# Spreading the B and C rows of the selective scans by TensorE instead of DMA, and moving the first block's injections

## The chip, the cores and the metric

The kernel runs on one core of a Trainium2 chip. Its engines are TensorE (PE), VectorE (DVE), ScalarE (ACT), GpSimd (POOL) and SyncE (SP, which only issues DMAs here). They run their own instruction streams and wait for each other by semaphores. The metric is the device time of one execution in microseconds, as a median over runs.

## The reference, cut to what matters

Two layers over 2048 tokens of width 128. The change touches the second layer's bidirectional Mamba block (inner width 256, 16 states, two directions "f" and "b"), which is computed side by side with that layer's attention and its mixture of eight experts.

```python
u, z = split(x @ Win.T); u = silu(causal_conv4(u)); dtr, B, C = split(u @ Wx.T)
dt = softplus(dtr @ Wdt.T + bdt)
# for each token t, channel d (256) and state n (16), in each direction:
h[d, n] = exp(dt[t, d] * A[d, n]) * h[d, n] + (dt[t, d] * u[t, d]) * B[t, n]
y[t, d] = sum_n h[d, n] * C[t, n]  +  u[t, d] * D[d]
out     = (y * silu(z)) @ Wout.T
```

B and C are 16 rows each per token, the same for all 256 channels.

## The kernel before

Three stages run one after the other: layer 0, the front stage (attention of the second layer, and the inputs of the Mamba block, which go to DRAM as dt, dt*u, u, z and the rows B, C), and the tail (the scans, the experts and the sums of all).

**The scans.** Tokens are cut into chunks of 512 (`CH`); two directions give 8 chunks n (`NN`). A scan tile is 128 partitions = 4 states x 32 channels, by 512 tokens. Input i = (n, b) is a chunk and a half b of the channels. Each i has 4 rounds (q = 0 to 3, a group of four states) of 4 tiles (j = 0 to 3, 32 channels). Tile k has r = k // 4 as its round. Per tile: ACT writes the decay exp(dt*A) into one of four PSUM banks (`spread_decay`); POOL makes the injection (dt*u)*B, two tiles at a time, into a ring of four (`inject`); DVE scans (L1709); the result is multiplied by C (`weigh`, on DVE, or on POOL for the tiles that `on_pool` names); ACT copies the last column of each tile for the next chunk (`keep`); PE adds the four states (`sums`, L1829), with a lag: the weighing of round r waits for the sums of round r - 2. The last chunk of each direction has nothing to keep. Round 0 to 3 (input 0) run at the end of the front stage as the "early" block; rounds r = 4 to 63 are the tail.

**B and C.** The row set m = 4n + q has four rows of B and four of C. Each must be on 32 partitions, to match the tile. `Inputs.load_bc` does that with 8 broadcast DMAs of 64 KB (L419) into one of five slots (`NBC`) of `bs` and `cs`. The row sets 0 to 4 are loaded in the front stage, the others in the tail, in rounds with r % 8 >= 4, for the chunk that follows. All are issued by SP, in program order with the loads of dt (L405), of dt*u (L405 too), of u and z (L411), of the experts' weights (L1359 to L1363) and the stores of their results (L1367). The inputs dt and dt*u of i + 1 are issued at the first round of i, once their buffer (two are used in turn) is free; SP stands behind each wait.

**Beside the scans.** PE and ACT share three PSUM banks (`ring`) for everything else: transposes and matmuls of the experts (T, H, Y), the projection of a chunk (O), and at the start of the tail the normed rows (N), the router's logits (L) and counts (C). A use takes the bank of the third use before it, once that was emptied. The order of the uses is one list over the rounds (`uses_beside`); ACT or DVE empties two to three rounds later, at fixed tiles.

**The start of the tail.** DVE adds the attention's output and takes its statistics, ACT standardizes 16 token tiles (`standardize`, L1479), PE turns them, ACT applies gain and bias (`normed`), PE makes logits, DVE chooses experts (`choose`) and places tokens (`place`), and POOL scatters rows by indirect DMA, one per two scan tiles (rounds 12 to 19). In these rounds and in 56 to 63 POOL weighs no tiles.

**The early block.** In the attention, unit u (0 to 255; 16 units make a step s) is: scores on PE, two exponentials on ACT (L853), weights times values on PE. DVE finds the maxima of a later step's scores beside it (L881). At the end of a step's maxima POOL splits them into three parts (`split_max`, L710 to L716), PE turns them, DVE copies them (`place_rows`, L895) and SP stores them into the queries (L597); the step's first scores wait for that. The maxima end at u = 234; from U0 = 235 the early block is scanned: POOL injects (L727), DVE scans (L941) and weighs (L949), POOL keeps (L733), PE sums (L1116). Its injections share two buffers, so that each waits for scans.

## Time and profile before

| | us |
|---|---|
| median of 3 runs | 1341.69 (1341.12 to 1343.34) |
| the profiled execution | 1339.88 |
| its span, first to last instruction | 1338.2 |
| DVE busy | 1205.2 (90%) |
| PE busy | 976.8 (73%) |
| ACT busy | 867.7 (65%) |
| POOL busy | 499.4 (37%) |
| tail stage | 883 to 1338 |

Busy shares are means over stages with different limits. A stage is read by stretches, and a stall by what ended it. Times of events are microseconds from the start of the span.

### The profile page before, as it was taken

The page shows a single profiled execution, that of the slowest core. Times are in us where ns is not written, and L with a number is a line of the kernel's source. Part 1 is how long each engine was busy: PE and PEld are TensorE (multiplying, and loading weights), DVE is VectorE, ACT ScalarE, POOL GpSimd, SP SyncE. Part 2 cuts the span into 40 slices and gives each one's busy share as a digit, 9 for nine tenths or more (in the row PEclk, how much of TensorE's full clock was granted, in tenths as well). Part 3 has the DMA queues.
Part 4 walks back from the last instruction along what each step waited for, and adds up shares of the span by engine and source line. Part 5 has one row for each costly group of instructions (what it writes and reads, how often), then busy time and mean ns, then how long its engine had stood idle before and what let it go on. Part 6 is the DMA issues. An engine that isn't in the chain of part 4 may idle for free. (4 is left out here: it accounts for less than half of the span.)

```text
span 1338.2 us, 18056 instructions
## 1 busy us (share of the span) xinstructions
PE 976.8 (73%) x5909; PEld 319.3 (24%) x5909; DVE 1205.2 (90%) x1759; ACT 867.7 (65%) x1298; POOL 499.4 (37%) x353
## 2 busy tenths in 40 slices
PE   2789996888888888888888888855433676767443
PEld 1443321111111111111111111122101344434111
DVE  7882667999999999999999999958999998989997
ACT  6445557777777777787877887757344655656531
POOL 5030113300000000000000012747698998988994
PEclk9889996999999999999999999885656867777565
DMA  3034333200000033000001100036467888797731
GB/s 100 0 129 151 132 126 128 73 1 1 1 29 18 12 64 64 29 24 16 7 17 33 33 17 1 2 88 162 85 151 152 192 215 199 181 210 183 190 81 34
DMA packets 88863, 111.47 MB, mean 83 GB/s; under 512 B 15603, under 2 KB 46122, under 8 KB 88770
## 3 DMA queue, kind: packets, MB, share of 16 engines
q1 hardware_dynamic: 87746, 108.22, 31.2%
q0 software_dynamic: 1024, 2.10, 0.6%
q8 instruction: 47, 0.77, 0.2%
q14 instruction: 46, 0.38, 0.1%
HBM read 84.43 MB, written 25.56 MB: 82 GB/s over the span
## 5 line engine op out<-in xcount | busy, mean ns | idle before, releaser
L881 DVE TENSOR_REDUCE at_mpart<-psum 128x1 f32<-128x512 f32 x1024 | 637.8, 684 | 44.1 <-PE psum L1058 40.9
L853 ACT ACTIVATE at_probs<-psum 128x1024 f32<-128x1024 f32 x512 | 495.3, 1021 | 146.4 <-PE psum L1088 145.6
L1453 POOL TENSOR_TENSOR t_inject<-shared 128x1024 f32<-128x1024 f32 x120 | 281.0, 2353 | 56.4 <-DVE psum L1709 23.5
L1101 PE MATMUL psum<-at_probs,at_vg 128*32 128x512 f32 x2048 | 276.5, 612 | 0.9 <-ACT at_probs L853 0.9
L1058 PE MATMUL psum<-at_ks,at_qs 56*128 56x512 bf16 x1024 | 203.1, 393 | 100.3 <-DVE at_mpart L881 99.6
L710 POOL CAST at_m<-at_mneg 128x16 bf16<-128x16 f32 x16 | 4.0, 251 | 574.5 <-DVE at_mneg L886 567.6
L1515 ACT ACTIVATE psum<-shared,aneg 128x512 f32<-128x512 f32 x240 | 164.5, 691 | 70.2 <-DVE t_hc L1641 56.5
L1829 PE MATMUL psum<-t_hc,stack 128*32 128x512 f32 x480 | 98.6, 906 | 137.7 <-DVE t_hc L1641 102.7
L1709 DVE TENSOR_TENSOR_SCAN psum<-psum,last,t_inject 128x512 f32<-128x512 f32 x149 | 184.0, 1273 | 1.1 <-ACT psum L1515 1.1
L1088 PE MATMUL psum<-at_qs,at_ks 59*128 59x512 bf16 x1024 | 157.9, 382 | 9.4 <-ACT at_probs L853 5.2
L1058 PEld LDWEIGHTS psum<-at_ks,at_qs 56*128 56x128 bf16 x1024 | 49.3, 93 | 424.5 <-DVE at_mpart L881 409.9
L1641 DVE TENSOR_TENSOR t_hc<-psum,shared 128x512 f32<-128x512 f32 (+1 forms) x121 | 112.9, 933 | 0.0
L1527 ACT ACTIVATE last<-psum 128x1 f32<-128x1 f32 x128 | 21.1, 165 | 137.4 <-DVE t_hc L1641 134.7
L1439 POOL TENSOR_TENSOR t_hc<-t_hp,shared 128x512 f32<-128x512 f32 x59 | 74.5, 1272 | 4.0 <-DVE t_hp L1709 3.9
L1088 PEld LDWEIGHTS psum<-at_qs,at_ks 59*128 59x128 bf16 x1024 | 50.3, 96 | 60.3 <-ACT at_probs L853 27.9
L1709 DVE TENSOR_TENSOR_SCAN t_hp<-psum,last,t_inject 128x512 f32<-128x512 f32 x43 | 54.6, 1270 | 9.2 <-ACT psum L1515 7.8
L1030 PE MATMUL psum<-mp_xm,mp_taps 128*128 128x512 f32 x128 | 62.7, 641 | 0.0
L696 POOL TENSOR_TENSOR shared<-shared 128x1024 f32<-128x1024 f32 x8 | 22.3, 2802 | 98.6 <-DVE shared L933 98.6
L1829 PEld LDWEIGHTS psum<-t_hc,stack 128*32 128x32 f32 x480 | 13.3, 134 | 190.2 <-issue 145.4
L1101 PEld LDWEIGHTS psum<-at_probs,at_vg 128*32 128x32 f32 x2048 | 40.5, 108 | 63.2 <-issue 60.1
L1783 PE MATMUL psum<-t_xT,t_w 128*128 128x128 f32 x184 | 36.4, 361 | 22.7 <-ACT t_xT L1486 21.2
L1824 PE MATMUL psum<-shared,diag 128*32 128x512 f32 x120 | 25.5, 937 | 21.1 <-DVE t_gated L1652 21.1
(248 smaller groups left out, 987.0 us busy)
## 6 DMA issues: line engine op xcount, KB each, us to landing
shared<-mp_dt_d SPq DMA_DIRECT2D x64, 256.0 KB, 5.9
shared<-mp_dtu_d SPq DMA_DIRECT2D x64, 256.0 KB, 9.3
shared<-mp_bc_d SPq DMA_DIRECT2D x256, 64.0 KB, 2.1
t_w<-in_w SPq DMA_DIRECT2D x46, 256.0 KB
mp_u_d<-shared SPq DMA_DIRECT2D x8, 512.0 KB, 4.8
mp_z_d<-shared SPq DMA_DIRECT2D x8, 512.0 KB, 4.6
mp_dt_d<-shared SPq DMA_DIRECT2D x8, 512.0 KB, 2.8
mp_dtu_d<-shared SPq DMA_DIRECT2D x8, 512.0 KB, 2.7
```

The lines of the kernel that those rows point to most:

```text
L853: act.activation(probs[:, u_ % 2, p, :], s_pair[p], ACT.Exp, scale=float(HD) ** -0.5).then_inc(probs_ready, 1)
L881: dve.reduce_max(mpart[:, s % 2, 2 * jp + b, i, kc:kc + 1], ring[x % 3], AX.X).then_inc(ring_free, 1)
L1030: mm = pe.matmul(out, S.taps[:, d, i, P * b:P * (b + 1)], xm[:, n % 2, i:i + CH], start=(i == 0), stop=(i == KC - 1))
L1058: pe.matmul(ring[z_ % 3], qs[half(b, DQ), buf, of_pair(jp, c * CH + i * P, P)], ks[half(b, DQ), buf, of_pair(jp, kc * CH, CH)], start=True ...
L1088: mm = pe.matmul(s_banks[p][b], ks[half(b, DM), g % 2, of_pair(p, kt * P, P)], qs[half(b, DM), g % 2, of_pair(p, c * CH, CH)], start=True, ...
L1101: mm = pe.matmul(o_bank[VW * j:VW * (j + 1), :], vg[:, g % 2, kt, j, :], probs[:, u_ % 2, j // 2, CH * (j % 2):CH * (j % 2 + 1)], start=(k ...
L1439: pool.tensor_tensor(hc[:, r % 2, j, :], hp[:, by_pool[k] % NHP, :], cs[:, (NQ * (i // NB) + q) % NBC, :], ALU.mult).then_inc(pool_weighed, 1)
L1453: pool.tensor_tensor(inject[:, k % NI:k % NI + 2, :], dus[:, i % 2, j:j + 2, :], bs[:, m % NBC, :].unsqueeze(1).to_broadcast([P, 2, CH]), ...
L1515: act.activation(decay[k % ND], dts[:, i % 2, j, :], ACT.Exp, scale=S.aneg[:, n // NCH, m:m + 1])\
L1641: dve.tensor_tensor(hc[:, r % 2, j:j + n, :], decays[:, j:j + n, :], cs[:, m % NBC, :].unsqueeze(1).to_broadcast([P, n, CH]), ALU.mult).th ...
L1709: dve.tensor_tensor_scan(h, decay[k % ND], inject[:, k % NI, :], last[:, k % PC:k % PC + 1] if n % NCH else 0.0, ALU.mult, ALU.add).then_i ...
L1829: mm = pe.matmul(y_bank[GC * j:GC * (j + 1), :], S.stack[:, :], hc[:, r % 2, j, :], start=False, stop=(q == NQ - 1), tile_position=(0, GC ...
```

## The change

In the front stage the early injections get eight buffers of their own (parts of buffers that are no longer used), and POOL makes them ahead, after the maxima of steps 12, 13 and 14. DVE's early scans and weighings are placed anew, and so are PE's early sums.

In the tail one DMA per chunk loads the 32 rows of B and C onto 32 partitions (`bc_rows`). PE multiplies them with a 0/1 matrix (`sel`, built once by POOL) into a bank of the ring, for B and for C of each row set (key S), and ACT copies the bank into the slot of `bs` or `cs` two rounds later. SP's broadcasts and their waits go; ACT waits instead for the slot to be free, and POOL and DVE wait for ACT's copy. In rounds 4 to 11 POOL also weighs tile 3 of the rounds where it did not. Several steps at the start of the tail come one tile later, and the scatters two tiles.

```diff
         first = Inputs(S)
+        early_in = [vg_all[:, 0:2 * CH], vg_all[:, 2 * CH:4 * CH]]
+        early_in += [t.rearrange("p k f -> p (k f)") for t in (S.taps[:, 0, :, :], S.taps[:, 1, :, :])]
+        early_in += [t.rearrange("p n f -> p (n f)")[:, 0:2 * CH] for t in (S.w_in[:, :, :], xm[:, :, :])]
+        early_in = [t.rearrange("p (j t) -> p j t", t=CH) for t in early_in]
+        early_in += [first.dts[:, 0, 0:2, :], first.dts[:, 0, 2:4, :]]
...
-        early_in = vg_all[:, 0:NJ * CH].rearrange("p (j t) -> p j t", t=CH)
...
         LAST_CONST = 2 + 2 * NB + SP4 + 1
+        EARLY_PAIRS = (0, 1), (2, 3, 4), (5, 6, 7)
...
                     pool.wait_ge(first_in[6 + q], 16 * 2 * SP4)
-                if p >= 2:
-                    pool.wait_ge(e_scanned, 2 * p - 2)
-                pool.tensor_tensor(early_in[:, j:j + 2, :], first.dus[:, 0, j:j + 2, :],
+                if p == 2:
+                    pool.wait_ge(prep_free, len(STEPS))
+                if p == 6:
+                    pool.wait_ge(e_decay, NE0)
+                pool.tensor_tensor(early_in[p], first.dus[:, 0, j:j + 2, :],
...
             for s in range(1, NSTEP):
-                if s == NSTEP - 1:
-                    for p in range(2):
+                if s >= NSTEP - 3:
+                    for p in EARLY_PAIRS[s - NSTEP + 3]:
...
                 early_keep(p)
-                if p + 2 < NE0 // 2:
-                    early_inject(p + 2)
...
                     dve.wait_ge(e_injected, k + 1)
-                    dve.tensor_tensor_scan(tile, tile, early_in[:, k % NJ, :], 0.0, ALU.mult, ALU.add).then_inc(e_scanned, 1)
+                    dve.tensor_tensor_scan(tile, tile, early_in[p][:, k % 2, :], 0.0, ALU.mult, ALU.add).then_inc(e_scanned, 1)
...
                     maxima(n)
-                if U0 <= u_ <= U0 + NE0 and (u_ - U0) % 2 == 0:
-                    p = (u_ - U0) // 2
-                    if p < NE0 // 2:
-                        early_scan(p)
-                    if p:
-                        early_weigh(p - 1)
+                if u_ == U0:
+                    early_scan(0)
+                    early_scan(1)
+                if u_ == U0 + 3:
+                    early_weigh(0)
+                if U0 + 3 <= u_ < U0 + 3 + NE0 - 4 and (u_ - U0 - 3) % 2 == 0:
+                    early_scan((u_ - U0 - 3) // 2 + 2)
+                    early_weigh((u_ - U0 - 3) // 2 + 1)
+                if u_ == U0 + 3 + NE0 - 4:
+                    early_weigh(NE0 // 2 - 1)
...
                     maxima(n)
-                if U0 + 7 <= u_ < U0 + 7 + 4 * NQ and (u_ - U0 - 7) % 4 == 0:
-                    early_sums((u_ - U0 - 7) // 4)
+                if u_ - U0 in (7, 11, 14, 17):
+                    early_sums((7, 11, 14, 17).index(u_ - U0))
...
             r, j = divmod(k, NJ)
-            return not SCATTER <= r < SCATTER + MOVE and not GATHER <= r < GATHER + MOVE and (j == 0 or j == 3 and r % 3 == 1)
+            return not SCATTER <= r < SCATTER + MOVE and not GATHER <= r < GATHER + MOVE and (j == 0 or j == 3 and (r % 3 == 1 or r < SCATTER))
...
 
+        def spread_at(r):
+
+            m = r // 8 * NQ + r % 8
+            return m if r % 8 >= 4 and NBC <= m < NN * NQ else None
+
         def uses_beside(r):
             keys = []
+            if (m := spread_at(r)) is not None:
+                keys += [("S", m, 0), ("S", m, 1)]
...
         hn2 = sb("hn2", [P, NCH, CH])
+        bc_rows, sel = sb("bc_rows", [BC, 2, CH]), sb("sel", [BC, 2 * NQ, P])
...
         dt_in, du_in, uz_in = ([sem(f"{n}_in{p}") for p in range(2)] for n in ("dt", "du", "uz"))
-        bc_in = [sem(f"bc_in{p}") for p in range(NBC)]
+        bc_in, sel_ready = [sem(f"bc_in{p}") for p in range(2)], sem("sel_r")
...
         def _(sp):
-            def load_bc(m):
-                n0, q0 = divmod(m - NBC, NQ)
-                done = PC * n0 + PB + NJ * (q0 + 1)
-                sp.wait_ge(injected, done - K0)
-                sp.wait_ge(pool_weighed, by_pool[done])
-                sp.wait_ge(dve_weighed, by_dve[done // NJ])
-                feed.load_bc(S, sp, m, bc_in[m % NBC])
+            def load_bc(n):
+                d, c = divmod(n, NCH)
+                if n >= 3:
+                    sp.wait_ge(side_full, USE["S", NQ * (n - 2) + NQ - 1, 1] + 1)
+                sp.dma_start(bc_rows[:, n % 2, :], S.bc_d[d][:, cols(c)]).then_inc(bc_in[n % 2], 16)
...
 
+            load_bc(1)
             for r in range(R0, NR):
                 i, rest = divmod(r, NQ)
+                if r % 8 == 0 and r // 8 + 1 < NN:
+                    load_bc(r // 8 + 1)
                 if rest == 0 and 2 <= i + 1 < NN * NB:
                     load_steps(i + 1)
-                if NBC <= r // 8 * NQ + NQ + r % 8 - 4 < NN * NQ and r % 8 >= 4:
-                    load_bc(r // 8 * NQ + r % 8)
...
             def numbering():
+                pool.tensor_copy(sel[:, :, :].rearrange("r x (s g) -> r (x s) g", g=GC),
+                                 S.ident[0:BC, 0:BC].unsqueeze(2).to_broadcast([BC, BC, GC])).then_inc(sel_ready, 1)
...
                 if j == 0 and m >= NBC:
-                    pool.wait_ge(bc_in[m % NBC], 16 * 2 * SP4 * (m // NBC))
+                    pool.wait_ge(emptied["act"], EMPTIED[USE["S", m, 1]][1])
...
                 if k % 2:
-                    if SCATTER <= r < SCATTER + MOVE:
-                        scatter((k - SCATTER * NJ) // 2)
+                    if 2 <= k - SCATTER * NJ < 2 + 2 * NT:
+                        scatter((k - SCATTER * NJ - 2) // 2)
...
                         .then_inc(xn_ready, 1)
+
+            def spread_states(m, o):
+                full("S", m, o)
+                if o == 0:
+                    n0, q0 = divmod(m - NBC, NQ)
+                    done = PC * n0 + PB + NJ * (q0 + 1)
+                    act.wait_ge(injected, done - K0)
+                    act.wait_ge(pool_weighed, by_pool[done])
+                    act.wait_ge(dve_weighed, by_dve[done // NJ])
+                act.activation((bs, cs)[o][:, m % NBC, :], bank("S", m, o), ACT.Copy).then_inc(emptied["act"], 1)
...
                         turned(s)
+                if m < 2:
+                    if (x_ := spread_at(r - 2)) is not None:
+                        spread_states(x_, m)
...
-                if k in (K0 + 17, K0 + 20):
+                if k in (K0 + 17, K0 + 21):
                     normed(0 if k == K0 + 17 else 2)
                     normed(1 if k == K0 + 17 else 3)
-                if K0 + 11 <= k < K0 + 11 + NCH:
-                    standardize(k - K0 - 11)
+                if K0 + 12 <= k < K0 + 12 + NCH:
+                    standardize(k - K0 - 12)
...
                 if m >= NBC:
-                    dve.wait_ge(bc_in[m % NBC], 16 * 2 * SP4 * (m // NBC))
+                    dve.wait_ge(emptied["act"], EMPTIED[USE["S", m, 1]][1])
...
                     variances()
-                if k == K0 + 8:
+                if k == K0 + 9:
...
-                if k in (K0 + 20, K0 + 23):
-                    logits(0 if k == K0 + 20 else 2)
-                    logits(1 if k == K0 + 20 else 3)
-                if k == K0 + 24:
+                if k in (K0 + 21, K0 + 24):
+                    logits(0 if k == K0 + 21 else 2)
+                    logits(1 if k == K0 + 21 else 3)
+                if k == K0 + 25:
                     choose()
-                if K0 + 28 <= k < K0 + 31:
-                    place[k - K0 - 28]()
+                if K0 + 29 <= k < K0 + 32:
+                    place[k - K0 - 29]()
...
                 return ring[x % R]
+
+            def spread_states(m):
+                n, q = divmod(m, NQ)
+                for o in range(2):
+                    out = take("S", m, o)
+                    if o == 0:
+                        pe.wait_ge(bc_in[n % 2], 16 * ((n + 1) // 2 if n % 2 else n // 2))
+                        pe.wait_ge(sel_ready, 1)
+                    pe.matmul(out, sel[:, NQ * o + q, :], bc_rows[:, n % 2, :], start=True, stop=True).then_inc(side_full, 1)
...
                 sums(r)
+                if (m := spread_at(r)) is not None:
+                    spread_states(m)
```

## Rows read from the trace of the kernel before

**Rows 1.** The page: busy us, share of the span and instructions of each engine.
```profile
PE 976.8 (73%) x5909; PEld 319.3 (24%) x5909; DVE 1205.2 (90%) x1759; ACT 867.7 (65%) x1298; POOL 499.4 (37%) x353
```
**Rows 2.** Tail by stretches: length; PE, PEld, DVE, ACT, POOL busy; clock; DMA share; GB/s.
```profile
883.00:960.60 77.60, 36.99 (x190) 21.04 (x190) 66.91 (x112) 39.22 (x90) 56.57 (x38) 0.60 0.58 131
960.60:1018.73 58.13, 22.15 (x91) 4.39 (x92) 58.13 (x61) 26.66 (x64) 52.84 (x32) 0.53 0.56 132
1018.73:1266.13 247.40, 158.79 (x874) 88.06 (x872) 232.71 (x220) 144.00 (x394) 225.11 (x120) 0.74 0.83 196
```
**Rows 3.** The same view: rounds 27, 35, 43, 51 and, undisturbed, round 30.
```profile
1065.36:1073.48 8.12, 6.68 (x47) 4.75 (x46) 6.53 (x7) 5.15 (x12) 5.89 (x4) 0.97 0.97 241
1118.53:1129.01 10.48, 9.67 (x53) 6.73 (x53) 5.79 (x6) 6.33 (x18) 6.48 (x5) 0.74 0.96 228
1174.54:1184.56 10.02, 8.36 (x51) 6.18 (x51) 6.51 (x8) 7.20 (x21) 5.20 (x4) 0.80 0.94 219
1230.61:1239.79 9.18, 8.91 (x50) 6.71 (x51) 6.53 (x6) 6.02 (x17) 5.90 (x4) 0.68 0.99 234
1086.96:1093.39 6.43, 3.97 (x32) 2.52 (x28) 6.43 (x7) 3.26 (x6) 6.43 (x4) 0.98 0.71 209
```
**Rows 4.** Timeline of SP's queue before round 28: start, length, line, transfer.
```profile
1044.18 7.32 SPq L419 DMA_DIRECT2D shared<-mp_bc_d  x16
...
1057.01 4.69 SPq L405 DMA_DIRECT2D shared<-mp_dtu_d  x4
```
**Rows 5.** The chain of waits, before round 44: start, length, what.
```profile
1171.18 10.82 DMA shared<-mp_dtu_d
```
**Rows 6.** The page's DMA issues: count, KB each, median us to landing.
```profile
shared<-mp_bc_d SPq DMA_DIRECT2D x256, 64.0 KB, 2.1
```
**Rows 7.** Timeline around the last step's start: start, length, instruction, [idle before].
```profile
832.77 1.06 POOL L716 TENSOR_TENSOR at_m<-at_mrem,at_m 128x16 bf16<-128x16 f32 x1
...
833.92 2.38 POOL L727 TENSOR_TENSOR at_vg<-shared 128x1024 f32<-128x1024 f32 x1
834.05 3.33 DVE L949 TENSOR_TENSOR xh<-xh,shared 128x1024 f32<-128x1024 f32 x1 [0.23 <-DVE xh L941]
...
837.31 0.21 DVE L895 COPY at_mrow<-psum 48x128 bf16<-48x128 bf16 x1
...
841.62 1.04 PE L1088 MATMUL psum<-at_qs,at_ks 59*128 59x512 bf16 x4 [3.69 <-DMA at_qs<-at_mrow]
842.32 1.94 ACT L853 ACTIVATE at_probs<-psum 128x1024 f32<-128x1024 f32 x2 [4.00 <-PE psum L1088]
...
847.83 1.94 ACT L853 ACTIVATE at_probs<-psum 128x1024 f32<-128x1024 f32 x2 [0.73 <-PE psum L1088]
...
853.26 1.19 DVE L949 TENSOR_TENSOR xh<-xh,shared 128x1024 f32<-128x1024 f32 x1
```
**Rows 8.** Busy time by stretches, in the last step's first units; columns as in rows 2.
```profile
840.00:844.00 4.00, 2.38 (x12) 0.33 (x12) 1.69 (x2) 1.68 (x2) 4.00 (x3) 0.58 0.01 4
```
**Rows 9.** The same view, of the logits' chain in rounds 8 and 9.
```profile
924.00:939.00 15.00, 14.14 (x64) 9.38 (x64) 11.64 (x16) 8.43 (x20) 12.12 (x7) 0.50 0.65 133
```
**Rows 10.** ACT's groups in the tail: busy us, mean ns of one, idle before.
```profile
L1479 ACT ACTIVATE t_x<-xn,t_shift,t_rstd 128x128 f32<-128x128 f32 x16 | 6.5, 481 | 0.0
...
L1531 ACT ACTIVATE t_y<-psum 128x512 f32<-128x512 f32 x4 | 2.1, 602 | 0.0
```
**Rows 11.** PE's groups, 960 to 1320 us: the projection's identity matmul, two instructions each.
```profile
L1802 PE MATMUL psum<-xn,ident 128*128 128x512 f32 x8 | 6.7, 927 | 0.0
```
**Rows 12.** Timeline of ACT and DVE in round 47.
```profile
1205.05 0.68 ACT L1515 ACTIVATE psum<-shared,aneg 128x512 f32<-128x512 f32 x1
...
1205.77 1.29 DVE L1709 TENSOR_TENSOR_SCAN psum<-psum,last,t_inject 128x512 f32<-128x512 f32 x1
```
**Rows 13.** DVE's groups in the tail: the weighing of one tile.
```profile
L1641 DVE TENSOR_TENSOR t_hc<-psum,shared 128x512 f32<-128x512 f32 x61 | 40.7, 668 | 0.0
```
**Rows 14.** The page's groups: POOL's weighing of one tile.
```profile
L1439 POOL TENSOR_TENSOR t_hc<-t_hp,shared 128x512 f32<-128x512 f32 x59 | 74.5, 1272 | 4.0 <-DVE t_hp L1709 3.9
```

## What I predict

> **What bounds the kernel now.** I read the page first: over the whole span DVE is busy 90% of the time and POOL only 37% [rows 1]. That average hides three stages, so I cut the span into stretches [rows 2]. Up to 883 us is layer 0 and the attention stage. After it comes the tail, in rounds of four scans, r = 4 to 63. In 960.60:1018.73 DVE is busy 58.13 of 58.13 us, so DVE alone is the bound there. In 883.00:960.60 DVE rests 77.60 - 66.91 = 10.7 us. In 1018.73:1266.13 it rests 247.40 - 232.71 = 14.7 us while POOL is busy 225.11, so the two pace each other with little room. The next question is where those 14.7 us lie. The starts of the scans show that most of it is in four rounds, r = 27, 35, 43 and 51, each the last before an odd input i is first read [rows 3]. They last 8.12, 10.48, 10.02 and 9.18 us where an undisturbed round lasts 6.43. DVE's rest in them is 1.59 + 4.69 + 3.51 + 2.65 = 12.4 us. The chain of waits says what ends it: the load of dt*u into `dus`, 10.82 us from its last issue to its landing before round 44; there is such a piece before each of the four [rows 5]. SP's own timeline says why it is late: before that load it issues 16 broadcasts of B and C in one go, 7.32 us, and dt*u itself takes 4.69 us to issue [rows 4].
>
> In the attention stage the change touches one place. At the start of the last step ACT waits 4.00 us for the scores [rows 7]. The order of events there is: POOL ends `split_max` (832.77 + 1.06); DVE's first early weighing takes 3.33 us, where a later one takes 1.19, because an early injection of POOL (2.38) began beside it; only then does DVE copy the maxima into `mrow` (837.31), SP store them, and PE start the scores (841.61, after 3.69 us idle). TensorE's clock falls during that idle: the granted clock of 840.00:844.00 is 0.58 [rows 8].
>
> **The change, part by part.**
>
> (a) Early injections ahead, front stage. All eight injections now run on POOL after the step maxima of steps 12, 13 and 14, into buffers that are free, beside DVE's maxima. `place_rows(15)` is in program order before the first early weighing, which moves from u = 237 to 238. It can then follow PE's turn of the maxima at about 834.2 instead of 837.31: 3.1 us sooner, and everything up to the scores is unchanged behind it (837.31 to 841.61 = 4.3 us, so the scores start near 838.5). PE would then idle about 0.6 us instead of 3.69, and I expect the clock to stay up; from ACT's 842.32 to 847.83 two units take 5.5 us, with 1.94 us of exponentials each and one copy of 0.6, so about 1 us comes back [rows 7, 8]. Sum: **-4.1 us**, bounds -2 and -5.5. DVE's other early work beside POOL's injections gets shorter too, but it is not what the stage ends on. The eight injections are not free by nature: 2.38 us each for POOL [rows 7]; they are hidden because POOL only waits for maxima there, and the first two already lie there today. If DVE's maxima were slowed by them, the cost would be that of a slowed weighing, 2.1 us each, at most 17; I see no such slowing beside the two that are there, so I take none.
>
> (b) B and C through TensorE, tail. Removed: 27 times 8 broadcasts of 64 KB from SP's queue (of the 256 on the page [rows 6]), with SP's waits for DVE and POOL in front of them. Each burst costs SP 7.32/16 = 0.46 us per DMA, 3.7 us per row set, and 13.8 MB of traffic. Added on SP: one 64 KB load per chunk, 7 in all. The stalls of 12.4 us should go: without the 16 broadcasts dt*u is issued at least 7 us sooner, and the expert weights that stand between them move up too. The largest stall is 4.7 us. What is late next is POOL or DVE themselves. I take **-12.4 us**, bounds 0 and -12.4.
>
> (c) What it adds. 54 matmuls (128x512, fp32) on PE; the nearest row is the identity matmul of the projection, 2 instructions of 927 ns each, 1.9 us; they are a mean over both clocks, so 1.1 to 1.9 is the span that I use [rows 11]. PE is busy 158.79 of 247.40 us in the middle stretch, so 4 row sets per 8 rounds at 2.3 to 3.8 us fit in work, if not in order. 54 copies on ACT; the nearest row is the PSUM copy of 128x512, 602 ns [rows 10]. ACT has room (144.00 of 247.40), but the place matters: both copies come in the burst between DVE's weighing and the next decays. In round 47 ACT's decay for tile 1 starts at 1205.05 and ends at 1205.73, and the scan of tile 1 starts at 1205.77 [rows 12]: no room at all. That is a round after one in which POOL weighs tile 3. After other rounds DVE has one more weighing, 0.67 us [rows 13], about one copy's worth of room. Of the 24 rounds with copies outside the start, the 4 of the scatter phase have that room and 6 lie in chunks without carried state, where the copy falls into ACT's wait. Of the 14 left, 5 follow a POOL round (0.55 each), and in the others I count 0.1 to 0.2 for the second copy. Together 2.8 + 0.7 to 1.8, so **+3.5 us**, bounds 0 and 28.8 (24 rounds of 1.2).
>
> (d) The start of the tail, r = 4 to 11. POOL first builds `sel` (a copy of 32x1024, estimated 1.2 us, half an injection's 2.38 [rows 7]), hidden because POOL rests there. POOL takes five more weighings, 1.27 us each, and DVE five fewer, 0.67 each [rows 13, 14]; DVE gains them only where it is busy throughout, about two of five, -1.2. Against that: four copies (2.4 us) get into ACT's queue in rounds 7 and 8, beside the 16 standardizations (6.5 us [rows 10]), where DVE already waits for decays, and the ring of three banks now makes PE's first logits wait for copies of ACT at k = 36 and 37. The chain of PE from 924 to 939 is busy 14.14 of 15.00 us at clock 0.50 [rows 9], and DVE waits for it already. Two spreads of row set 7 (3.8 us at half clock) come into that chain, ahead of the logits. Laying the order out by hand with these durations, the scans of round 8 start some 3 us later, and the logits 4 to 6 us later, less what DVE gets done meanwhile. Sum **+3.0 us**, bounds -1.2 (all hidden) and +5. The moves by one tile (standardize, shifts, logits, choose, place, scatter) only follow the later data; the scatter is one pair later, and the rows of x are still loaded sooner because the broadcasts of round 20 are gone from SP's queue. I cost them at nothing; without that cover the scatter would be 3.5 us late, with PE's first transpose.
>
> TensorE's clock decides part of (c) and (d). The row says that PE can be 94% busy for 15 us and stay at half, 1.2 GHz [rows 9]; I use half clock in the start. The Trainium skill, "TensorE: Matmul & The Clock Gate", section "What's actually happening", has the clock follow how busy the array has lately been, and by it the 12 added wide matmul passes of rounds 5 to 7 should lift the clock to full, 2.4 GHz. By that rule the sum would be that of the first rival below. The trace does not bear it out for the narrow logits.
>
> **Sum.** -4.1 - 12.4 + 3.5 + 3.0 = -10.0 us. The profiled execution took 1339.88 us (span 1338.2 and 1.7 around it), 1.8 under the median of 1341.69. It would become 1329.9, and the median **1331.7 us**. The bounds that I hold likely give 1326 to 1338.
>
> **Rivals.**
> The start is free and the copies hide. PE's clock rises when the spreads keep it busy, so the chain of 924 to 939 halves, and ACT does its copies while it waits for DVE. For it: ACT is busy only 58% of the middle stretch [rows 2]. Against it: the round with no room. -5.0 - 12.4 - 1.2 = -18.6, that is 1323 us.
> The stall stays. If the dt*u load is late through its own transfer (10.82 us to land; DMA share 0.97 in round 27 [rows 3, 5]) and not through SP's queue, (b) gives nothing: -4.1 + 3.5 + 3.0 = +2.4, 1344 us. Against it: the even inputs have the same transfer and no stall, and the broadcasts stand only before the odd ones.
> Slower: the copies of ACT take the place of the stall. Mechanism: in every round with spreads, both copies lie between DVE's weighing and the decays for the next scans, and the ring of three banks adds PE to that loop. Price up to 1.2 us in each of 24 rounds, 28.8 in all, with the start at +5: -4.1 - 12.4 + 28.8 + 5 = +17.3, 1359 us. It decides from (4.1 + 12.4 - 3.0)/24 = 0.56 us per round, nearly one copy. The scan at 1205.77 speaks for it [rows 12]; that most rounds have one weighing more on DVE speaks against it.
>
> **Chances.** Forecast 0.60, free start 0.15, stall stays 0.15, slower 0.10. 0.2% is 2.7 us, about what a measurement of this kernel can tell from no change: faster is below 1339.0, slower above 1344.4. Faster: the first two, 0.75. The stall that stays falls on the border, two thirds of it within: with the forecast's tail 0.13 same, 0.12 slower. For 8 in 10 the range goes from just under the free case, 1322, to just over the stall that stays, 1345.
>
> **What would show it.** Right: the scores of the last step wait about 1 us, not 4, and the clock stays at 1.00 through 840 to 848; rounds 27, 35, 43 and 51 last 6.3 to 6.6 us; no broadcast in the tail; in rounds such as 47 DVE idles 0.5 us for a decay; rounds 6 to 10 are some 4 us longer. Wrong: the four rounds still wait for dt*u (the stall stays), all rounds with spreads are 1 us longer (slower), or the granted clock at the start of the tail is 1.00 (free start). The forecast fails most easily on the start, where three engines wait for each other.

## The result and the profile after

The changed kernel takes 1330.07 us (median of 4 runs, 1328.24 to 1332.02), against 1341.55 beside it (1341.12 to 1343.34): 0.9909 times the time before, 95% interval 0.9894 to 0.9924. It is 11.5 us faster, and lies within 1.7 us of the forecast of 1331.7. A later set of runs of the same kernel (e12) gave 1331.20, ratio 0.9924 [0.9897, 0.9952].

The profiled execution took 1332.02 us, the slowest of its four, with a span of 1330.3; so a comparison of profiles shows 7.9 us less, not 11.5. The page gives the engines' busy time, two groups and the traffic. They answer to [rows 1] and [rows 6]:

```profile
PE 1036.7 (78%) x6017; PEld 340.5 (26%) x6017; DVE 1196.1 (90%) x1754; ACT 892.0 (67%) x1352; POOL 503.1 (38%) x359
...
DMA packets 78831, 97.77 MB, mean 73 GB/s; under 512 B 12259, under 2 KB 42778, under 8 KB 78738
...
L1789 PE MATMUL psum<-t_bc_rows,t_sel 32*128 32x512 f32 x108 | 79.9, 877 | 0.0
```

PE has 60 us of work more and ACT 24, and over the whole span neither is full. DVE has 9.1 us less. Its 16 early scans took 27.0 us, four of them 3.1 to 3.5 us each with an injection of POOL beside them, and take 1.2 us each now, the first weighing is back to its own length, and five weighings of the tail went to POOL (37.5 us for 56, where 61 took 40.7); a part of that comes back in operations that POOL now holds up in the start. The broadcasts of the tail are gone from the page; 13.7 MB less is moved (the page of before has 111.47 MB).

The tail by stretches, as [rows 2] (length; busy PE, PEld, DVE, ACT, POOL; clock; DMA share; GB/s), cut at the starts of rounds 4, 12, 20 and 56, and under it rounds 27, 35, 43 and 51, as [rows 3]:

```profile
879.50:961.21 81.71, 47.50 (x194) 23.60 (x196) 67.13 (x107) 43.26 (x99) 61.41 (x42) 0.58 0.47 104
961.21:1018.89 57.68, 35.07 (x111) 8.70 (x112) 57.68 (x60) 27.39 (x67) 51.94 (x32) 0.57 0.41 97
1018.89:1258.01 239.12, 191.57 (x945) 98.18 (x945) 233.02 (x219) 159.91 (x430) 225.91 (x120) 0.79 0.69 161
```
```profile
1065.43:1071.88 6.45, 4.74 (x32) 2.97 (x31) 6.45 (x7) 3.66 (x9) 6.45 (x4) 1.00 0.33 78
1116.92:1123.36 6.44, 5.70 (x19) 2.93 (x20) 5.79 (x7) 5.01 (x16) 6.44 (x5) 0.50 0.28 60
1171.66:1178.09 6.43, 5.68 (x25) 3.72 (x26) 6.43 (x8) 4.41 (x13) 5.90 (x4) 0.51 0.33 66
1225.24:1231.69 6.45, 6.21 (x35) 4.24 (x35) 6.45 (x7) 4.11 (x12) 6.45 (x4) 0.70 0.33 70
```

In the middle stretch DVE rests 6.1 us where it rested 14.7. The four rounds that waited for dt*u take 25.8 us together where they took 37.8. The start, rounds 4 to 11, is the loser: 81.71 us, where the same eight rounds took 75.13 before (starts of their scans, 885.46 to 960.59), with 14.6 us of rest.

The first scores of the last step, in the timeline (start, length, instruction, [idle before and releaser]), answer to [rows 7], and the three stretches behind them to [rows 8]:

```profile
831.22 1.06 POOL L721 TENSOR_TENSOR at_m<-at_mrem,at_m 128x16 bf16<-128x16 f32 x1
...
832.60 0.21 DVE L900 COPY at_mrow<-psum 48x128 bf16<-48x128 bf16 x1 [0.34 <-PE psum L1075]
832.74 1.21 DVE L954 TENSOR_TENSOR xh<-xh,shared 128x1024 f32<-128x1024 f32 x1
...
836.92 0.60 PE L1097 MATMUL psum<-at_qs,at_ks 59*128 59x512 bf16 x4 [0.55 <-DMA at_qs<-at_mrow]
...
837.41 1.94 ACT L858 ACTIVATE at_probs<-psum 128x1024 f32<-128x1024 f32 x2 [0.65 <-PE psum L1097]
```
```profile
834.00:838.00 4.00, 2.92 (x28) 0.62 (x24) 4.00 (x4) 3.35 (x5) 1.74 (x1) 1.00 0.04 9
838.00:842.00 4.00, 2.93 (x24) 0.54 (x16) 4.00 (x5) 4.00 (x6) 2.61 (x2) 1.00 0.00 0
842.00:846.00 4.00, 4.00 (x38) 0.95 (x36) 2.05 (x2) 2.25 (x3) 1.10 (x1) 1.00 0.00 0
```

From POOL's `split_max` to the copy of the maxima there are 0.3 us now, not 3.5. The weighing (L954) takes 1.21 us, not 3.33, and stands behind the copy. ACT waits 0.65 us instead of 4.00, and the clock stays up.

For a sum that leaves out what an execution does ahead of the early block (the profiles differ by 3 us there, with kernels whose code is the same up to it), I count from the start of the last exponential of unit 234. The lengths of rounds are the distances of the first scans of DVE. In us:

| stretch | before | after | after, second profile (e12) |
|---|---|---|---|
| last exponential of unit 234 to the tail's first scan | 58.95 | 54.55 | 54.54 |
| round 4 | 10.11 | 10.95 | 11.17 |
| rounds 7 to 10 | 34.60 | 39.31 | 37.84 |
| rounds 11 and 12 | 21.70 | 22.08 | 22.08 |
| rounds 27, 35, 43, 51 | 37.80 | 25.76 | 25.75 |
| the other rounds of 27 to 55 | 162.96 | 166.83 | 164.93 |
| last exponential of unit 234 to the end | 511.7 | 505.4 | 501.6 |

### The profile page after: what moved, and what is told of

The parts are those of the page before. It is cut to its first block and busy times, and to the rows that moved or that the text cites. A ratio compares the mean times of both kernels' runs of the same rounds, so it can differ in the third digit from the quotient of the medians.

```text
span 1330.3 us, 18174 instructions
## 1 busy us (share of the span) xinstructions
PE 1036.7 (78%) x6017; PEld 340.5 (26%) x6017; DVE 1196.1 (90%) x1754; ACT 892.0 (67%) x1352; POOL 503.1 (38%) x359
## 5 line engine op out<-in xcount | busy, mean ns | idle before, releaser
L1110 PE MATMUL psum<-at_probs,at_vg 128*32 128x512 f32 x2048 | 273.7, 606 | 0.7 <-ACT at_probs L858 0.6
L1740 DVE TENSOR_TENSOR_SCAN psum<-psum,last,t_inject 128x512 f32<-128x512 f32 x146 | 181.0, 1276 | 4.4 <-ACT psum L1543 4.1
L1869 PE MATMUL psum<-t_hc,stack 128*32 128x512 f32 x480 | 95.4, 878 | 96.9 <-DVE t_hc L1672 55.7
L1672 DVE TENSOR_TENSOR t_hc<-psum,shared 128x1024 f32<-128x1024 f32 (+1 forms) x116 | 109.7, 946 | 0.0
L1457 POOL TENSOR_TENSOR t_hc<-t_hp,shared 128x512 f32<-128x512 f32 x64 | 80.6, 1270 | 2.5 <-DVE t_hp L1740 2.4
L1789 PE MATMUL psum<-t_bc_rows,t_sel 32*128 32x512 f32 x108 | 79.9, 877 | 0.0
L1740 DVE TENSOR_TENSOR_SCAN t_hp<-psum,last,t_inject 128x512 f32<-128x512 f32 x46 | 58.5, 1271 | 1.6 <-POOL t_inject L1471 0.8
L1823 PE MATMUL psum<-t_xT,t_w 128*128 128x128 f32 x184 | 34.0, 344 | 11.9 <-ACT t_xT L1514 11.9
```

The costliest lines, as they stand in the source:

```text
L1110: mm = pe.matmul(o_bank[VW * j:VW * (j + 1), :], vg[:, g % 2, kt, j, :], probs[:, u_ % 2, j // 2, CH * (j % 2):CH * (j % 2 + 1)], start=(k ...
L1457: pool.tensor_tensor(hc[:, r % 2, j, :], hp[:, by_pool[k] % NHP, :], cs[:, (NQ * (i // NB) + q) % NBC, :], ALU.mult).then_inc(pool_weighed, 1)
L1672: dve.tensor_tensor(hc[:, r % 2, j:j + n, :], decays[:, j:j + n, :], cs[:, m % NBC, :].unsqueeze(1).to_broadcast([P, n, CH]), ALU.mult).th ...
L1740: dve.tensor_tensor_scan(h, decay[k % ND], inject[:, k % NI, :], last[:, k % PC:k % PC + 1] if n % NCH else 0.0, ALU.mult, ALU.add).then_i ...
L1789: pe.matmul(out, sel[:, NQ * o + q, :], bc_rows[:, n % 2, :], start=True, stop=True).then_inc(side_full, 1)
L1869: mm = pe.matmul(y_bank[GC * j:GC * (j + 1), :], S.stack[:, :], hc[:, r % 2, j, :], start=False, stop=(q == NQ - 1), tile_position=(0, GC ...
```

## The experiments

**Each half alone.** e1 takes all hunks of the diff up to the end of the front stage, e2 all those of the tail.

> The kernel before with only the front-stage part of the change (early injections ahead, early scans, weighings and sums placed anew); the tail is that of before. My theory: the last step's scores come 3.1 us sooner and the clock stays up, so -4.1 us (-3 to -5.5): in the trace of the changed kernel the step from u = 235 to the tail's first scan is 4.4 us shorter. Rival: what the front gains, the tail's start takes back, because it waits for something else; then 0 us.

e1: 1339.58 us, ratio 0.9971 [0.9953, 0.999]; median 3.1 us under the 1342.68 beside it. The stretch up to the first scan is 54.54 us as in the full change, so its gain of 4.4 is the front's alone. But round 4 takes 11.24 us, not 10.11. Round 4 is long in nine of the ten profiles of kernels with the front's part (10.8 to 11.3), and in none of the four others (10.11). The timeline shows what differs: PE's first 16 transposes of the tail. First the full change, where round 4 took 10.95, then the run e8 below, the one of the ten that took 10.11:

```profile
877.04 3.16 PE L1875 MATMUL psum<-ident,at_v 128*128 128x128 f32 x16 [1.95 <-PEq L60]
```
```profile
878.31 1.94 PE L1875 MATMUL psum<-ident,at_v 128*128 128x128 f32 x16 [1.95 <-PEq L60]
```

ACT's first copies of the tail and its decays stand behind these transposes. The windows around them, of the full change and then of e8, give their clocks:

```profile
877.00:879.00 2.00, 1.96 (x12) 1.99 (x13) 0.00 (x0) 1.75 (x3) 1.97 (x1) 0.64 0.34 69
```
```profile
878.30:880.30 2.00, 1.99 (x18) 2.00 (x19) 0.00 (x0) 2.00 (x4) 2.00 (x1) 1.00 0.31 75
```

PE rests 1.95 us ahead of them by both. In nine of the ten profiles with the front's part the granted clock is at half (1.2 GHz) behind that rest and the 16 transposes take 3.0 to 3.5 us; in the four others they take 1.94. Why the clock differs there was not tried. About 1 us of the front's 4.4 is handed back. The tail takes more back in the profile of e1: rounds 27, 35, 43 and 51, which still wait for dt*u, take 39.45 us together instead of 37.80, and from the last exponential of unit 234 to the end this profile is only 0.9 us shorter than that of the kernel before. So the rival has a part of it; the median says -3.1, with an interval from 1.3 to 6.3.

> The kernel before with only the tail's part of the change (B and C by TensorE and ScalarE, POOL's five more weighings, the steps moved by a tile). My theory: the parts add up, so this is the whole change less the front: the traces give rounds 4 to 11 +6.0 us, rounds 12 to 55 -8.1 us, so about -2 us in that pair of executions, and -7 by the medians (-11.5 + 4.4). Rival: the parts do not add, because the clock's phase at the tail's start depends on when the front ends; then anything from -2 to -10.

e2: 1333.87 us, ratio 0.9942 [0.9923, 0.9961], 8.8 us under the kernel beside it. With e1 that makes -11.9, and both together measured -11.5: the halves add up, as far as intervals of 5 us each can tell. Rounds 27, 35, 43 and 51 are undisturbed here. Rounds 7 and 8 take 10.18 and 8.05 us, as in the full change (10.19 and 8.06; 9.10 and 7.20 before). So the start's loss belongs to the tail's part.

**Is it SP's queue or the bytes?** Both edit `Feed.load_bc` of the kernel before, for the row sets of the tail; e3 issues one broadcast of 64 KB of the eight (7/8 of the rows are left out), e4 moves all bytes with four DMAs of 128 KB, one per group of 32 partitions, for B and C together.

```diff
                 row = off + SP4 * q + s
+                if m >= self.NBC and (s or off):
+                    continue
```
```diff
+        if m >= self.NBC:
+            both = S.shared[:, 20 * CH:(20 + 2 * self.NBC) * CH].rearrange("p (o n t) -> p o n t", o=2, t=CH)
+            rows = S.bc_d[d].rearrange("(o x) t -> x o t", o=2)
+            for s in range(SP4):
+                x = SP4 * q + s
+                sp.dma_start(both[GC * s:GC * (s + 1), :, m % self.NBC, :],
+                             rows[x:x + 1, :, c * CH:(c + 1) * CH].to_broadcast([GC, 2, CH])).then_inc(done, 16)
```

> The kernel before, where in the tail only one of the eight broadcasts of each row set is issued (the rest of B and C is left out, so the scans run on old rows). Nothing is added on PE or ACT. Theory SP's queue: the four stalls go and nothing else changes, -12.0 us (-11 to -13). Rival, the dt*u transfer is late by itself: the stalls shrink only as far as the DMA share falls, less than -6. Either way it is the price of what the change adds: the change's tail gains less than this by the start and by the rounds 40 and 48.

> The kernel before, where each row set in the tail is loaded by four DMAs of 128 KB (B and C in one) instead of eight of 64 KB: the same bytes, half the issues. Theory SP's queue: a row set costs SP 1.8 us less, the burst of two 3.7 us less, so the stalls of 1.6, 2.7 and 3.5 us nearly go and 4.7 us shrinks to about 1: -8 to -11 us. Theory of the transfer itself (bytes): the stalls stay, 0 to -2 us.

e3: 1329.21 us, ratio 0.9896 [0.9878, 0.9914]. e4: 1329.28 us, ratio 0.9898 [0.9879, 0.9916]. The two are the same, and each is as fast as the whole change. e4 gained more than its theory had (-13.4 us, where it said -8 to -11): the largest stall went whole, too. In both, rounds 27 to 34 take 51.49 us (53.17 before) and rounds 4 to 11 stay at 75.1. SP's queue before round 28 and the window of round 27, in e4:

```profile
1043.16 4.85 SPq L428 DMA_DIRECT2D shared<-mp_bc_d  x8
...
1053.60 4.87 SPq L405 DMA_DIRECT2D shared<-mp_dtu_d  x4
```
```profile
1066.89:1073.34 6.45, 5.00 (x32) 3.07 (x32) 6.45 (x7) 3.65 (x9) 6.45 (x4) 0.95 1.04 322
```

Counted from the start of round 24, SP begins to issue dt*u after 6.5 us here and after 11.4 before (1057.01 - 1045.57, [rows 4]). The DMA share of the round is 1.04, higher than the 0.97 of [rows 3], and there is no stall. So the cause was the place of the load in SP's queue, not the traffic. A burst for two row sets takes 4.85 us instead of 7.32, that is 0.61 per DMA of 128 KB against 0.46 per DMA of 64 KB.

**Front and wide loads together.** e5 is the front's part and e4's edit, with none of the tail's part.

> The kernel before with the front-stage part of the change and, in place of the tail's part, four DMAs of 128 KB per row set instead of eight of 64 KB. Theory: the two gains are in different stages and add: 0.9971 x 0.9898, -17.6 us against the kernel before, some 6 us faster than the change. Rival: the clock's phase at the tail's start takes part of it back, as the fronts' shift may lengthen round 10; then -12 to -14 us.

e5: 1324.50 us (1323.82 to 1325.71), ratio 0.9864 [0.9841, 0.9888], against 1342.24 beside it. Its interval lies below that of the full change. Its four rounds, 27, 35, 43 and 51:

```profile
1062.37:1068.82 6.45, 5.01 (x32) 3.08 (x32) 6.45 (x7) 3.65 (x9) 6.45 (x4) 0.95 1.09 311
1113.87:1120.30 6.43, 5.69 (x30) 3.73 (x31) 5.79 (x7) 5.00 (x16) 6.43 (x5) 0.71 0.84 225
1165.81:1172.24 6.43, 5.69 (x24) 3.73 (x25) 6.43 (x8) 4.41 (x13) 5.96 (x4) 0.50 0.95 269
1218.33:1224.77 6.44, 6.18 (x32) 4.21 (x33) 6.44 (x6) 4.12 (x12) 6.44 (x4) 0.60 0.41 81
```

It has the gain of both parts of the change and pays nothing to PE and ACT. It has the lowest median of all the runs; against e4 alone (1329.28) it is 4.8 us lower, and the two intervals just overlap.

**The start without spreads.** e6 is the changed kernel, with the first three row sets (m = 5 to 7) by DMA as before, and spreads from m = 8.

```diff
-                return m if r % 8 >= 4 and NBC <= m < NN * NQ else None
+                return m if r % 8 >= 4 and 8 <= m < NN * NQ else None
...
+                if 5 <= r < 8:
+                    ...
+                    feed.load_bc(S, sp, r, first_bc[r - 5])
```

> The changed kernel, but row sets 5, 6 and 7, which fall in rounds 5 to 7, are loaded by the old broadcasts (24 DMAs); spreads begin at row set 8. POOL's extra weighings and the moves by a tile stay. Theory spreads: the +6.6 us of rounds 4 to 11 (75.13 to 81.71) come from the six matmul pairs and six copies there; they fall to 76 to 78 and the kernel is some 4 us faster than the changed one. Rival, the moves by a tile and POOL's weighings: rounds 4 to 11 stay at 80 to 82.

e6: 1326.42 us, ratio 0.9884 [0.9862, 0.9907]. Rounds 4 to 11 take 75.42 us (81.71 with the spreads): rounds 7 and 8 are back at 9.13 and 7.20, round 9 takes 6.27, round 10 takes 10.59. So the spreads of three row sets cost 6.3 us against the first profile, and 5.1 against that of e12 below (80.47). In this run too rounds 40 and 48 are long, 9.44 and 8.52 us.

**Which part of the spread costs?** Of the changed kernel, e7 makes the matmuls 64 columns wide instead of 512, e8 the copies, e9 both; the rest of the columns is left out. All orders and waits stay. e9 has both lines:

```diff
-                    pe.matmul(out, sel[:, NQ * o + q, :], bc_rows[:, n % 2, :], start=True, stop=True).then_inc(side_full, 1)
+                    pe.matmul(out[:, 0:64], sel[:, NQ * o + q, :], bc_rows[:, n % 2, 0:64], start=True, stop=True).then_inc(side_full, 1)
...
-                act.activation((bs, cs)[o][:, m % NBC, :], bank("S", m, o), ACT.Copy).then_inc(emptied["act"], 1)
+                act.activation((bs, cs)[o][:, m % NBC, 0:64], bank("S", m, o)[:, 0:64], ACT.Copy).then_inc(emptied["act"], 1)
```

> The changed kernel, but each spread's matmul makes only 64 of 512 columns (the other columns of B and C are left as they stand in the bank, so the scans run on wrong rows). ACT's copies stay whole. Theory PE: the stalls of rounds 40 and 48 (2.4 and 0.9 us) are PE's time at half clock in a ring of three banks; they go, and rounds 4 to 11 lose 1 to 3 of their 6.6 us. Theory ACT: the copies' place is what costs; nothing changes by more than 1 us but what the clock does.

> The changed kernel, but ACT copies only 64 of 512 columns of each spread (the rest of B and C is not renewed, so the scans run on old rows). PE's matmuls stay whole. Theory ACT: rounds 6 to 8 of the start lose DVE's waits for decays, 2 to 3 of the 6.6 us, and DVE's rest in round 47 goes from 0.5 back to 0.3. Theory PE: rounds 40 and 48 stay some 2 us longer whenever the clock is at half there, and round 10 stays above 10 us.

> The changed kernel with both the 54 spread matmuls of PE and the 54 copies of ACT cut to 64 of their 512 columns; 7/8 of the spread B and C columns are left out, so the result is only for its time. All orders and waits stay. Theory (width: the work itself costs, the hand-offs do not): what is left of the spreads' cost falls nearly to nothing; rounds 4 to 11 take 75.4 to 76.6 us, as where the first three row sets come by DMA (75.42), rounds 40 and 48 take 7.0 to 7.1 us, the median is 1325.5 to 1327. Rival (order: the ring of three banks and the four steps between PE, ACT, DVE and POOL cost, however narrow the work is): rounds 4 to 11 stay at 78 us or above, near the 78.67 of the run with narrow copies alone, and the median stays at 1328 or above.

e7: 1330.90 us, ratio 0.9909 [0.9884, 0.9933]. e8: 1328.48, ratio 0.9902 [0.9877, 0.9927]. e9: 1325.34, ratio 0.9866 [0.985, 0.9883]. The lengths of the rounds that differ, in us, with the granted clock where it matters:

| round | before | after | e12 | e6 | e7 | e8 | e9 |
|---|---|---|---|---|---|---|---|
| 7 | 9.10 | 10.19 | 10.18 | 9.13 | 10.19 | 9.44 | 9.44 |
| 8 | 7.20 | 8.06 | 8.05 | 7.20 | 8.05 | 7.31 | 7.31 |
| 9 | 9.88 | 9.06 | 9.06 | 6.27 | 8.69 | 9.82 | 7.94 |
| 10 | 8.42 | 12.00 (0.50) | 10.55 (0.65) | 10.59 (0.62) | 10.55 (0.66) | 10.55 (0.66) | 12.01 (0.50) |
| 24 | 7.04 | 7.03 | 7.02 | 7.02 | 7.77 (0.56) | 8.97 (0.60) | 7.05 |
| 32 | 6.32 | 6.33 | 7.43 (0.67) | 6.33 | 6.32 | 6.34 | 6.34 |
| 40 | 7.02 | 9.39 (0.58) | 7.19 (1.00) | 9.44 (0.62) | 7.02 | 7.24 | 7.33 (0.61) |
| 48 | 7.04 | 7.93 (0.57) | 7.02 (0.76) | 8.52 (0.58) | 7.89 (0.56) | 7.04 | 7.04 |

Rounds 7 and 8 answer to the copies alone: both lose 0.75 us when the copies are narrow, and nothing when the matmuls are. A copy of 512 columns takes 597 ns in the median, one of 64 takes 223, and there are two: 0.75. The windows of rounds 7 and 8, first after, then e9:

```profile
907.47:917.65 10.18, 6.69 (x16) 2.08 (x16) 6.13 (x9) 10.03 (x26) 7.13 (x5) 0.50 0.08 19
917.65:925.71 8.06, 6.44 (x16) 2.08 (x16) 6.65 (x7) 5.92 (x14) 7.70 (x5) 0.50 0.92 190
```
```profile
910.41:919.85 9.44, 4.02 (x16) 1.84 (x16) 6.32 (x9) 9.28 (x26) 7.15 (x5) 0.50 0.10 20
919.85:927.17 7.32, 5.20 (x21) 2.62 (x21) 6.55 (x8) 5.18 (x15) 7.32 (x5) 0.50 0.90 191
```

In round 7 ACT is the bound, busy 10.03 of 10.18 us: four decays and sixteen standardizations, with the copies on top. In round 8 ACT is busy only 5.92 of 8.06 us, but DVE waits 1.21 us for a decay that stands behind both copies (0.66 in the kernel before, 0.77 in e8).

For rounds 24 and 48 it is not enough to make one of the two narrow: e7 takes 7.77 and 7.89 us, though its theory had the stalls gone, and e8 takes 8.97 in round 24. With both narrow (e9) no such round takes over 7.33 us.

e9 fell between its two outcomes. Its median is just under the 1325.5 of the theory (the width costs), and rounds 40 and 48 are back at 7.33 and 7.04, nearly as that says. But rounds 4 to 11 take 79.27 us, as the rival says. The profile is of the slowest of its four executions (1329.59 us; the others took 1324.86 to 1325.77), and 1.45 us of it is round 10 at half clock. Without these, rounds 7 to 10 would be 35.2 us: 2.6 less than the full change at the same clock (37.84), but 2.1 over e6 (33.19), which has the same order and no spreads there. So in the start the width of the spreads is the larger part, 2.6 of 4.7 us, and some 2 us stay with their hand-offs. This split rests on single profiles.

**POOL's five extra weighings.** e10 is the changed kernel with the old rule in `on_pool`; e11 is e5 with the new rule.

```diff
-            ... and (j == 0 or j == 3 and (r % 3 == 1 or r < SCATTER))
+            ... and (j == 0 or j == 3 and r % 3 == 1)
```

> The changed kernel with the weighings of rounds 4 to 11 divided between POOL and DVE as in the kernel before (POOL's five more undone, DVE does them again). Theory (the prediction's): DVE is the one that gains where it is busy throughout, so undoing this costs about 1.2 us: rounds 4 to 11 take 82 to 83.5 us, the median is 1331.3. Rival: POOL's weighings of 1.27 us stand in front of its injections in the start and hold up DVE's scans, so undoing them gives 1 us or more: rounds 4 to 11 below 81, the median below 1329.3. If neither shows, rounds 4 to 11 take 81.3 to 82.0.

> The version with the front's part and the broadcasts by DMA, 4 of 128 KB per row set, and now with the changed kernel's division of the weighings in rounds 4 to 11 (POOL five more). Theory: the same -1.2 us where no spreads stand in the way: rounds 4 to 11 take 75.1 us instead of 76.32, the median is 1323.3. Rival (POOL's place in front of the injections): rounds 4 to 11 take 77.3 us or more, the median 1325.5. The comparison holds the first rule without PE's and ACT's added work.

e10: 1331.24 us, ratio 0.9919 [0.9899, 0.994]. Rounds 4 to 11 take 79.87 us, which looks like the rival; but round 12 is 0.6 us longer, and round 10 has a clock of 0.66. Rounds 4 to 12 take 88.11 us, and the same in e12, where round 10 ran at 0.65. e11: 1326.92 us, ratio 0.9869 [0.9845, 0.9893]; rounds 4 to 11 take 76.37 us (e5 76.32), rounds 4 to 12 84.0 (e5 84.6). Neither the gain that I expected nor the rival's loss is there. The rounds show what POOL's rule does: round 12 takes 7.64 us with it and 8.24 without (7.63 and 8.23 in e11 and e5), round 11 takes 14.43 with it and 13.78 without (13.57 and 13.47). In the changed kernel one round loses what the next gains. The medians cannot tell e11 from e5: its runs spread over 5 us. I call the rule worth nothing that was measured here, at most 0.6 us.

**The same kernel again.** e12 is the changed kernel, unedited.

> The changed kernel once more, unedited, for a second profiled execution. Theory: what rounds 10, 24, 32, 40 and 48 cost hangs on whether TensorE is granted full or half clock in them, which differs between executions of one kernel: the rounds that are long here (round 10 at 12.0 or 10.55 us; 24, 32, 40, 48 at 7.0 or 8 to 9.4) are others than in the first profile, each long one has a granted clock of 0.5 to 0.62, and rounds 7 and 8 stay at 10.19 and 8.06 us in both. Rival: their lengths are fixed by the order of the instructions, so round 10 is 12.00, round 40 is 9.39 and round 48 is 7.93 us again. The median is 1330 by both.

e12: 1331.20 us, ratio 0.9924 [0.9897, 0.9952]. Its column stands in the table above. Rounds 7 and 8 are the same to 0.01 us. Round 10 is 10.55 us, round 40 is 7.19 and round 48 is 7.02; instead round 32 takes 7.43, and each of the long ones has the low clock. So these lengths belong to the clock of the execution, not to the order alone. The spreads that precede round 40, in the timeline, first of the first profile, then of e12:

```profile
1148.91 3.78 PE L1789 MATMUL psum<-t_bc_rows,t_sel 32*128 32x512 f32 x4
...
1151.02 0.60 ACT L1508 ACTIVATE shared<-psum 128x512 f32<-128x512 f32 x1 [0.80 <-PE psum L1789]
1151.51 0.69 ACT L1543 ACTIVATE psum<-shared,aneg 128x512 f32<-128x512 f32 x1
...
1152.23 1.29 DVE L1740 TENSOR_TENSOR_SCAN psum<-psum,last,t_inject 128x512 f32<-128x512 f32 x1 [0.81 <-ACT psum L1543]
1152.72 0.60 ACT L1508 ACTIVATE shared<-psum 128x512 f32<-128x512 f32 x1 [0.44 <-PE psum L1789]
```
```profile
1151.89 2.15 PE L1789 MATMUL psum<-t_bc_rows,t_sel 32*128 32x512 f32 x4
...
1153.22 0.60 ACT L1508 ACTIVATE shared<-psum 128x512 f32<-128x512 f32 x1
1153.72 0.69 ACT L1543 ACTIVATE psum<-shared,aneg 128x512 f32<-128x512 f32 x1
...
1154.43 2.47 DVE L1740 TENSOR_TENSOR_SCAN psum<-psum,last,t_inject 128x512 f32<-128x512 f32 x2
```

At half clock the spreads take 3.78 us. ACT reaches its copy before PE is done, waits 0.80, the decay behind it is late, and DVE's scan waits 0.81. In e12 their mean clock is 0.91, they take 2.15 us, and in these lines nobody waits.

The same pair of spreads, the last ahead of rounds 24, 32, 40 and 48, tells in other traces too which of these rounds is long. In six profiles with wide matmuls (the first, e12, e2, e6, e8, e10) it ran at half clock throughout, in 3.78 us, seven times, and the round behind it took 7.43 to 9.44 us each time. In the other 17 it took 1.98 to 3.31 us, and only one round behind it was long, round 48 of the first profile. That round takes as long with narrow matmuls (7.93, 7.89 in e7), and in both DVE waits half a microsecond for PE's sums. The mean clock of a round tells less: round 32 took 6.33 us at 0.66 in e6 and 7.43 at 0.67 in e12.

## Why the prediction was right, and where not

**(a) The front: right.** Predicted -4.1, measured -4.4 up to the tail's first scan, by the mechanism named: the scores at 836.92, the wait 0.65 us, the clock at 1.00. What it missed is the 1 us that comes back in round 4, where PE at half clock makes the first transposes longer. The median of e1, -3.1, holds both, and the longer wait for dt*u of that kernel.

**(b) SP's queue: right in kind and size.** Predicted -12.4, measured -12.0. Rounds 27, 35, 43 and 51 take 6.43 to 6.45 us. The rival that the stall stays, through the transfer itself, fell: e4 moves every byte, has a higher DMA share, and no stall.

**(c) The added work: the sum right, its place wrong.** Predicted +3.5, measured +3.9 in one profile and +2.0 in the other (the other rounds of 27 to 55). The step that failed is that five rounds after a POOL round would pay 0.55 us each, since there ACT's decay had no slack [rows 12]. Round 47 is such a round. Its timeline in the changed kernel:

```profile
1199.77 0.60 ACT L1508 ACTIVATE shared<-psum 128x512 f32<-128x512 f32 x1
1199.83 2.47 DVE L1740 TENSOR_TENSOR_SCAN psum<-psum,last,t_inject 128x512 f32<-128x512 f32 x2 [0.47 <-ACT psum L1543]
1200.24 0.71 ACT L1543 ACTIVATE psum<-shared,aneg 128x512 f32<-128x512 f32 x1
```

DVE does idle half a microsecond, as I said it would. But it had idled 0.3 us in that round before, and the round is 6.42 us long against 6.32: the price is 0.1, not 0.55 (the same in round 23). POOL is busy for the whole of the round in both kernels, 6.32 and 6.42 us, so a wait of DVE cost little there. I had read the wait ahead of one scan and taken it for time on the path, without subtracting the rest that the round had already. The cost lies where I counted none: in the first round of a block of eight, when the clock is low in it. That is the loop of the slower rival (PE through the ring, then ACT, then the decays), in one or two of the rounds 24, 32, 40 and 48 of a profile instead of in all 24. What decides in which of them the clock is low was not tried. That the sum comes near the forecast is luck: neither the five rounds at 0.55 nor the nine at 0.1 to 0.2 (0.9 to 1.8 us together, not 0.7 to 1.8) are what was measured.

**(d) The start: right in direction, too small.** Predicted +3.0 with +5 as the bound. Rounds 4 to 12 measured +6.0 and +4.7. Of these about 1 us is the front's, in round 4. Of the rest, rounds 7 to 10 are +3.2 where round 10 has its partly full clock and +4.7 where it has half, and rounds 11 and 12 are +0.4. The mis-sized term is this one. Rounds 7 and 8 pay the width of ACT's two copies in full, 0.75 us each, and the logits' chain comes two spreads later, as laid out: in round 10 DVE waits 2.0 us for the logits at half clock and 0.4 in e12. That POOL's five weighings would give 1.2 us back was wrong (e10, e11). The moves by a tile, costed at nothing, change how long DVE takes for the choice of experts, as the next lines show; what they cost or give by themselves was not measured.

DVE's timeline of the choice of experts, which falls in round 10, beside POOL's, in the first profile of the changed kernel and then in e12:

```profile
939.83 2.34 POOL L1471 TENSOR_TENSOR t_inject<-shared 128x1024 f32<-128x1024 f32 x1 [1.13 <-DVE psum L1740]
939.86 2.45 DVE L1619 TENSOR_TENSOR t_pick<-t_lg,t_top 128x128 f32<-128x128 f32 x1
```
```profile
941.48 2.38 POOL L1471 TENSOR_TENSOR t_inject<-shared 128x1024 f32<-128x1024 f32 x1
941.70 2.31 DVE L1621 TENSOR_TENSOR t_pick<-t_pick,t_prio 128x128 f32<-128x128 f32 x1
```

The first of these two operations took 0.69 us in the kernel before, the second 0.29. Here one of them starts just behind an injection of POOL and ends with it. All four operations of the choice took 1.66 us together before and take 3.41 and 3.67 here. They take 3.3 to 4.0 us in every kernel with the steps moved by a tile, e6 (no spreads in the start) and e10 (POOL's old rule) among them, and 1.65 or 1.66 in e1, e3, e4 and e5, where the steps stand as before (2.24 in e11, with POOL's new rule). So 1.8 to 2.0 us of DVE's time in round 10 go with the moved order. This is not their net price: e6, with them, takes 16.86 us for rounds 9 and 10 together, where the kernel before takes 18.30. In the start every delay moves such operations against POOL's, so its sum is no plain sum of durations.

Round 11 is 1 us longer as well (14.44 us, 13.47 before), and its operations are hit in other places: `t_ends` takes 1.88 us (0.81 before) and `t_passed` 1.66 (0.33), while `t_rank` takes 0.29 (2.36). With POOL's old rule the round takes 13.78 us (e10), so 0.65 of it goes with the five weighings, and round 12 gives 0.6 back.

**The sum.** The four terms made -10.0. Measured one by one they make -6.5 in the first profile and -9.7 in the second; from the last exponential of unit 234 to the end these show -6.3 and -10.1, and the medians -11.5 and -11.4. Most of the 3.8 us between the two is the low clock of rounds 10, 40 and 48 in the first (1.45 + 2.2 + 0.9 us), less that of round 32 in the second (1.1). The forecast of the median came out 1.6 us too high. That lies within what single executions of one kernel differ by (1328.24 to 1332.02 here), and I cannot give it a place. With (c) in the wrong place and (d) too small, so near a median is in part luck.

The free start did not come: in the profiles the granted clock of rounds 5 to 8 is 0.50 in the changed kernel, with PE busy 6.4 to 6.7 us of rounds 7 and 8, and in round 9, which PE fills, it is 0.50 and 0.52.

## What to carry to other kernels

When a load is late, look at what its queue issues in front of it before looking at its bytes. Halving the count of DMAs at the same bytes (e4, a dozen lines) gave as much as the whole change, which moves the work to two other engines, and without their cost. Work put on a "free" engine costs its full length in the few rounds where that engine is the bound or its clock is low, so look for these rounds and not for its mean share.

## What the runs showed of the hardware

**TensorE's clock as a source of spread.** Between two executions of one kernel round 40 took 9.39 or 7.19 us, with 0.58 or 1.00 as the granted clock. In the Trainium skill, "TensorE: Matmul & The Clock Gate", section "What's actually happening", the point at which the clock rises varies between runs of one kernel. The traces agree: round 10 ran at 0.50 in one and at 0.65 in the other.

**A vector operation held up by POOL.** An operation of DVE with two inputs in SBUF took 2.45 us beside an injection of 2.34, and 0.31 us in e8, where it began 0.11 us ahead of the injection. The Trainium skill, "SBUF — State Buffer", section "Who interferes with whom", has an exclusive lock on the ports that DVE and GpSimd share, for such an operation while GpSimd reads SBUF, and the second to start waits for the whole of the first. The trace agrees: DVE starts 0.03 us behind POOL and ends 0.14 us after it. DVE's first early weighing before (3.33 us, [rows 7]) fits too: it started 0.13 us behind POOL's injection and ended 1.08 after it, nearly its own length of 1.19. In e8 the operation behind it, at 2.31 us, started 0.23 us behind the injection and ended 0.14 after it. The 0.69 us of the kernel before fit as well: a weighing of POOL ran beside the operation's first 0.54 us.

**What a DMA cost on its queue does not follow its size.** A broadcast of 128 KB occupied SP for 0.61 us, one of 64 KB for 0.46. Of the loads of 256 KB, in the kernel before, ahead of round 28, the four of dt occupied SP for 1.76 us and the four of dt*u right behind them for 4.69.
